# Longer transfer times and margins in a planned instruction order, and six bursts of value products a group for seven

## The reference

```python
x = x + 0.5 * ffn(layernorm(x))
x = x + attn(layernorm(x))
x = x + 0.5 * ffn(layernorm(x))
# ffn:  r = sigmoid(xr @ W_r.T); k = xk @ W_k.T; out = r * (relu(k)**2 @ W_v.T)
#       xr, xk mix each token with the one before it
# attn: q, k, v of 16 heads; rope(q), rope(k); softmax(causal(q k^T / 4)) @ v; @ W_proj + b_proj
```

## Time and profile before

| what | value |
| --- | --- |
| median of 3 runs | 3101.86 us (3099.11 to 3105.67) |
| the profiled execution's own time | 3100.36 us |
| its span, first to last instruction | 3098.6 us |
| PE busy / weight loads busy | 2952.3 us (95%) / 1671.2 us (54%) |
| DVE, ACT, POOL busy | 2497.6 (81%), 2219.9 (72%), 1590.9 us (51%) |

### The profile page before, as it was taken

One profiled execution on the slowest core, in us unless ns is written; L12 is line 12 of the kernel. 1 busy time (PEld: TensorE's weight loads), 2 busy tenths in 40 slices (PEclk: granted clock), 3 DMA queues, 4 the chain that ended last, 5 costly groups with the idle time before them and its releaser, 6 DMA issues.

```text
span 3098.6 us, 56240 instructions
## 1 busy us (share of the span) xinstructions
PE 2952.3 (95%) x18245; PEld 1671.2 (54%) x18245; DVE 2497.6 (81%) x7302; ACT 2219.9 (72%) x4802; POOL 1590.9 (51%) x2190
## 2 busy tenths in 40 slices
PE   6899999999999999999999999999999999999997
PEld 4454455554555545555555555555555555555444
DVE  3888788787878888888888878888888888888872
ACT  4477677777767777777777777777777777777764
POOL 5455455555545555545555555554555555555323
PEclk9899999999999999999999999999999999999999
DMA  3432342333423323333333423323333433433321
GB/s 99 80 78 66 72 96 60 94 75 69 98 59 94 84 67 97 77 84 73 95 74 75 97 61 93 86 75 87 77 87 74 96 71 74 100 67 78 79 63 39
DMA packets 202585, 245.49 MB, mean 79 GB/s; under 512 B 68405, under 2 KB 104245, under 8 KB 202293
## 3 DMA queue, kind: packets, MB, share of 16 engines
q1 hardware_dynamic: 202293, 241.90, 33.5%
HBM read 53.48 MB, written 51.38 MB: 34 GB/s over the span
## 4 chain that ended last, share of the span: by engine, by line
PE 57%; DVE 14%; DMA 8%; ACT 6%; SPq 5%; POOL 5%; issue 4%; POOLq 0%; ACTq 0%; DVEq 0%
PE ps_y L947 11%; PE ps_s L916 11%; PE ps_m L926 9%; PE ps_d L1000 5%; PE ps_d L1003 5%; PE ps_d L1006 5%; DMA sw_sb<-qb_sb 5%; DVE ps_m L1155 4%; PE ps_d L1012 4%; SPq L824 3%; ACT pt_sb L1042 3%; PE ps_d L993 3%; DMA out<-x_sb 3%; DVE mx_sb L1158 2%; DVE ka_sb L1180 2%
## 5 line engine op out<-in xcount | busy, mean ns | idle before, releaser
L1042 ACT ACTIVATE pt_sb<-ps_s 128x512 f32<-128x512 f32 (+1 forms) x3039 | 1455.7, 491 | 703.6 <-PE ps_s L916 675.1
L1155 DVE CUSTOM_DVE_ANT_0 ps_m<-ps_m,mask_sb 128x128 f32<-128x128 f32 (+3 forms) x2048 | 993.7, 497 | 227.7 <-PE ps_m L926 208.8
L926 PE MATMUL ps_m<-kr_sb,qr_sb 96*128 96x512 bf16 (+3 forms) x3072 | 1001.2, 329 | 69.5 <-DVE mx_sb L1155 62.3
L916 PE MATMUL ps_s<-qr_sb,kr_sb 99*128 99x512 bf16 (+1 forms) x3039 | 995.9, 330 | 26.9 <-ACT pt_sb L1042 17.4
L1158 DVE TENSOR_REDUCE mx_sb<-ps_m 128x1 f32<-128x512 f32 x1024 | 700.3, 684 | 91.2 <-PE ps_m L926 83.9
L1287 POOL TENSOR_SCALAR_AFFINE_SELECT pt_sb<-pt_sb 128x512 f32<-128x512 f32 x512 | 337.8, 660 | 580.3 <-ACT pt_sb L1042 578.4
L947 PE MATMUL ps_y<-pt_sb,v_sb 128*32 128x512 f32 (+3 forms) x6144 | 591.9, 495 | 2.9 <-POOL pt_sb L1287 1.9
L916 PEld LDWEIGHTS ps_s<-qr_sb,kr_sb 99*128 99x128 bf16 x3039 | 292.4, 96 | 446.6 <-issue 234.8
L926 PEld LDWEIGHTS ps_m<-kr_sb,qr_sb 96*128 96x128 bf16 x3072 | 302.1, 98 | 378.3 <-DVE mx_sb L1155 111.3
L1000 PE MATMUL ps_d<-ka_sb,wk_sb 128*128 128x256 f32 x1024 | 313.2, 393 | 8.7 <-DVE ka_sb L1180 5.8
L1012 PE MATMUL ps_d<-axn_sb,wqk_sb 128*128 128x256 f32 x1024 | 310.5, 388 | 3.9 <-ACT axn_sb L1084 3.8
(11 more groups left out here) (96 smaller groups left out, 3496.5 us busy)
## 6 DMA issues: line engine op xcount, KB each, us to landing
kr_sb<-part_sb SPq DMA_DIRECT2D x378, 128.0 KB, 3.4
qr_sb<-part_sb SPq DMA_DIRECT2D x378, 128.0 KB, 4.0
y_way<-yt_sb SPq DMA_DIRECT2D x128, 256.0 KB, 2.3
sw_sb<-qb_sb SPq DMA_DIRECT2D x496, 64.0 KB, 2.3
x_sb<-x SPq DMA_DIRECT2D x64, 256.0 KB, 3.3
yn_sb<-y_way SPq DMA_DIRECT2D x64, 256.0 KB
den_sb<-r_way SPq DMA_DIRECT2D x64, 256.0 KB
out<-x_sb SPq DMA_DIRECT2D x64, 256.0 KB, 2.3
```

What stands on the lines that cost most here:

```text
L916: eng.matmul(score_bank(slot)[:, 0:width], kr_sb[0:KR + NP, n % RS, j, kb * P:(kb + 1) * P], qr_sb[0:KR + NP, n % RS, j, q0:q0 + width], s ...
L926: eng.matmul(ps_m[:, u % NM, 0:width], qr_sb[0:KR, n % RS, j, i * P:(i + 1) * P], kr_sb[0:KR, n % RS, j, piece * QC:piece * QC + width], s ...
L1042: eng.activation(pt_sb[:, buffer, j, column:column + width], score_bank(slot)[:, 0:width], ACT.Exp, scale=SCALE).then_inc(exped, 1)
L1155: eng.tensor_tensor_reduce(ps_m[:, u % NM, 0:width], ps_m[:, u % NM, 0:width], mask_sb[:, m0:m0 + width], 1.0, -3e38, ALU.add, ALU.max, be ...
```

## The change

The list gets other numbers, and the bursts another grouping:

- `BURSTS`: the first two ticks of a group form one burst, as the others already do.
- `TAKES`: the times after which a DMA's result is taken to be there grow: `r_swap` 3600 to 7000, `store` 2500 to 5000, `load` 3800 to 7000, `m_rows` 2500 to 3000, `y_out` 3500 to 8000, `y_back` 2700 to 4500, `y_in` 4500 to 9000, and for `rows` and `part` 4900 to 7000.
- `MARGIN`: from slot 192 to slot 3024 a step is ready only so many ns after its inputs are due: PE 0, ACT 200, DVE and POOL 400, SP 1500.
- A step that follows another on the same engine no longer waits for that one's `done` but for the time at which the engine is free again (names with `+`): `f_x1`, `f_k1`, `f_r1`, `a_x1`, `r_b1`, and the steps of `rows` and `part` among themselves.

```diff
-BURSTS = [(0,), (1,), (2, 3), (4, 5), (6, 7), (8, 9), (10, 11)]
+BURSTS = [(0, 1), (2, 3), (4, 5), (6, 7), (8, 9), (10, 11)]
...
-             "a_xn": (477, 645), "a_vc": (477, 645), "a_bias": (1222, 1330), "r_b0": (356, 530), "r_b1": (356, 530), "r_swap": (240, 3600),
+             "a_xn": (477, 645), "a_vc": (477, 645), "a_bias": (1222, 1330), "r_b0": (356, 530), "r_b1": (356, 530), "r_swap": (240, 7000),
...
-             "r_low": (1170, 1500), "store": (60, 2500), "load": (60, 3800), "h_fin": (700, 900), "h_T": (130, 400), "h_copy": (156, 330),
-             "h_rows": (240, 2500), "m_fin": (900, 1000), "m_T": (130, 400), "m_copy": (157, 330), "m_rows": (60, 2500),
-             "y_copy": (477, 645), "y_out": (120, 3500), "y_recip": (159, 300), "y_back": (60, 2700), "y_in": (120, 4500),
+             "r_low": (1170, 1500), "store": (60, 5000), "load": (60, 7000), "h_fin": (700, 900), "h_T": (130, 400), "h_copy": (156, 330),
+             "h_rows": (240, 2500), "m_fin": (900, 1000), "m_T": (130, 400), "m_copy": (157, 330), "m_rows": (60, 3000),
+             "y_copy": (477, 645), "y_out": (120, 8000), "y_recip": (159, 300), "y_back": (60, 4500), "y_in": (120, 9000),
...
-            s("DVE", "f_k1", p, 0.62, t, ("f_k0", p, 0))
+            s("DVE", "f_k1", p, 0.62, t, ("f_k0+", p, 0))
...
-                  (f"rows{t - 1}", n if t else -1, 0))
+                  (f"rows{t - 1}+", n if t else -1, 0))
...
+    MARGIN = {"PE": 0, "ACT": 200, "DVE": 400, "POOL": 400, "SP": 1500}
...
-            if early > slot or not self.ready(now, after) or e != "PE" and rank[0] == 2 and self.TAKES[name][0] > room:
+            if early > slot or not self.ready(now - self.margin(e, slot), after) or e != "PE" and rank[0] == 2 and self.TAKES[name][0] > room:
...
-            pace, seen = self.TAKES.get(key[0], (240, 4900))
+            pace, seen = self.TAKES.get(key[0], (240, 7000))
             self.at[e][slot].append(key)
             self.slots[key] = slot
+            self.done[key[0] + "+", key[1]] = now + pace
             self.done[key] = now + seen
...
+    def margin(self, e, slot):
+
+        return self.MARGIN[e] if BSLOTS <= slot < self.nb * BSLOTS - GSLOTS else 0
...
+                at += self.margin(e, slot)
```

More of the change, by code:

```diff
@@ L152, in describe @@
             s("ACT", "f_x0", p, 0.36, t, ("f_rstd", p, 4))
-            s("ACT", "f_x1", p, 0.36, t, ("f_x0", p, 0))
+            s("ACT", "f_x1", p, 0.36, t, ("f_x0+", p, 0))
             s("PE", "f_T", p, 0.5, t, ("f_x1", p, 2))
@@ L157, in describe @@
             s("DVE", "f_k0", p, 0.62, t, ("f_dif", p, 2), ("f_V", p - 2, 1))
-            s("DVE", "f_k1", p, 0.62, t, ("f_k0", p, 0))
+            s("DVE", "f_k1", p, 0.62, t, ("f_k0+", p, 0))
             s("DVE", "f_r0", p, 0.46, t, ("f_k1", p, 0))
-            s("DVE", "f_r1", p, 0.46, t, ("f_r0", p, 0))
+            s("DVE", "f_r1", p, 0.46, t, ("f_r0+", p, 0))
             s("PE", "f_K", p, 4, t, ("f_k1", p, 3))
@@ L181, in describe @@
                 s("ACT", "a_x0", i, 0.36, t, ("a_rstd", i, 4))
-                s("ACT", "a_x1", i, 0.36, t, ("a_x0", i, 0))
+                s("ACT", "a_x1", i, 0.36, t, ("a_x0+", i, 0))
                 s("PE", "a_T", i, 0.5, t, ("a_x1", i, 2))
@@ L196, in describe @@
                     s("ACT", "r_b0", i, 0.36, t, ("r_QK", i, 1), ("r_low", i - 2 if i >= NCH + 2 else -1, 1))
-                    s("ACT", "r_b1", i, 0.36, t, ("r_b0", i, 0))
+                    s("ACT", "r_b1", i, 0.36, t, ("r_b0+", i, 0))
                     s("SP", "r_swap", i, 3.2, t, ("r_b1", i, 1), ("r_add", i - 1 if i > NCH else -1, 1))
@@ L211, in describe @@
                 if n == 0:
[L212 removed]
+                    s("SP", f"part{t}", n, 1, FIRST + t, (part, NCH // 2 - 1, 2), (f"part{t - 1}+", n if t else -1, 0))
                 s("SP", f"rows{t}", n, 1.6, max(FIRST, at - 2 * GSLOTS + (20 if n == 1 else 1) + 3 * t), (part, last, 2),
[L214 removed]
+                  (f"rows{t - 1}+", n if t else -1, 0))
             if n == 0:
@@ L448, in place_early @@
         for key, slot in self.slots.items():
-            self.done[key] = (slot - SWITCH) * self.TICK + self.TAKES.get(key[0], (240, 4900))[1]
+            self.done[key] = (slot - SWITCH) * self.TICK + self.TAKES.get(key[0], (240, 7000))[1]
             self.done[key[0] + "+", key[1]] = self.done[key] - 3 * self.UNIT
```

## The result

The changed kernel takes 3075.63 us (3071.78 to 3078.87, 4 runs), the kernel before 3100.49 (4 runs): a ratio of 0.9921 [0.9897, 0.9946], 25 us less where 65 were forecast. The lines of after are 7 higher than those of before (916 is now 923, 926 is 933, 1155 is 1162, 1158 is 1165, 1209 is 1216). The profiled execution took 3078.87 us.

A forecast was written before the change was run, and what follows sets the result against it. PE was taken as the bound, with holes made by other engines and transfers. Bursts -14, swap -42, `y_out` -4, clock -8, margins -9 and latency +12 gave -65: 3036 us, range 3005 to 3090.

The forecast's parts named there:

- The transfers: Longer swap times end DVE's waits for swapped halves, and PE's waits for the maxima behind them: -42, between 0 and 84.5 us.
- the one that proves it wrong: Sign against the prediction: DVE's wait for the swap goes, but PE's time per image does not.
- The bursts: Merging a group's first two ticks saves PE 0.24 us in each of 64 groups: 14 us, between 0 and 15.
- Rival (a): Only the bursts count; swaps still land late or the hole moves to POOL's cosine: 3068 to 3083, say 3078; chance 0.20.
- The margins (-9): Margins on ACT, DVE, POOL and SP shorten small waits on neighbours that reach PE: -9 us, between 0 and -45.
- The added latency (+12): Later placement in the list makes some PE slots lose their dense unit: +12 us, between 0 and +70.
- the 20 that were named: Sign against the prediction: PE's waits for lines 1000, 1003 and 1006 grow beyond 20 us.
- rival (b): Slower: later placements empty PE's slots of dense units, 4.5 a group costing 130 us: 3155; chance 0.08.
- no cost: `m_rows`, planned 2.0 us later from a place some 8 us ahead of its use, was to cost nothing.
- The clock (-8): Part of PE's 16 us of full speed missing from 300 to 1100 us returns: -8, between 0 and -16.
- The one event of the forecast: Swap issued at 313.38 us: DVE stands 6.79 us, PE idles 4.17, clock then lower, 3 us more from 320 to 330.
- The tail (0, -3 to +6): Last image's projections move behind the last burst, but scores end sooner by as much: 0, between -3 and +6 us.

The follow-up runs named there:

- the lightened kernels: DVE takes each maximum over half its columns: kernel after 3015.85 us, the same with seven bursts 3012.96, kernel before 3038.02.
- steps without meaning: `HEARD_PE`, when PE's results count as seen, changed from 200 by 10 or 20 ns, order only: old list moved 47 and 82 us, new up to 47.
- the bursts alone: Kernel before with six bursts a group, its list laid out anew by the old times: 3288.51 us, 1.0628 of before.
- six bursts at 210: Changed kernel with `HEARD_PE`, when PE's results count as seen, 210 ns for 200: 3056.83 us, 0.9859 of before.
- seven at 190: Changed kernel with seven bursts and `HEARD_PE`, when PE's results count as seen, 190 ns for 200: 3024.26 us, 0.9773 of before.
- three draws: `HEARD_PE` at 190, 200 and 210 ns in each list: old list's mean 3143.7 us, new list's 86 (seven bursts) and 74 (six) below.

## Why the prediction was wrong

**The transfers: right in what goes, wrong in what it is worth.** The forecast asked for under 15 us of DVE's wait for the swap (0.9) and 0.99 to 1.00 of clock from 300 to 1100 us (1.00); both came. It asked for under 20 us of PE's idle time for DVE and 181 us for an image's scores; 38.9 and 183.2 came. The step that failed is "nearest to PE's own 45.8 us on DVE, which is how much of DVE's 70.0 us reached it. I take 42". It took nearly all of PE's idle time for DVE as made by transfers, and let it go without asking what DVE would do then. By the timelines 26 to 37 of the 46.3 us did stand beside a wait of DVE for a DMA, and all of those went; by the lightened kernels it was some 27, and 19 of them went. What the forecast put at nothing came in their place: 38.9 us of waits for a DVE that is busy. Measured on PE, the term is 7. The sentence that DVE has 16% free was read as room; but the share is a mean, and before the holes of after DVE is busy for 96%. That is nearly the case which the forecast itself named as the one that proves it wrong: DVE's wait went, and PE's time for an image hardly moved (185.1 to 183.2).

By the Trainium skill ("DMA: Bandwidth & Descriptors", section "Anatomy of one DMA") the fixed cost of about 2.0 us and the bytes leave nothing for longer times to gain. The runs part the two questions: the waits that this fit does not see were real and are gone, and what that is worth in time no run shows by itself: `r_swap` alone made the kernel 2.8% slower, within what steps without meaning do to that list.

**The bursts: 14 us only at an order laid out for them.** 1.64 us for 16 records is right, and at the order of after the two single bursts cost 15 us more, as forecast. What failed is "The copies, DMAs and selects are not moved by it": the change lays the list out anew, and PE's new pace moves all of it. Against the list laid out for seven, six are worth +53, +5 and -21: no sign; and at an order laid out for seven they cost 7 and 20. Rival (a), "Only the bursts count", gave 3078, near the time measured, but its premise fell: the swaps did not land late, the hole did not move on to POOL's cosine (189.0 to 29.4 us), and the list alone gives the gain. That its number came so near is luck.

**The margins (-9)** are not to be seen: without them the time is the same within the intervals. **The added latency (+12)** is not either: PE waits 1.9 us for the key product's input, where it was 5.6, and no other product comes near the 20 that were named. So rival (b) fell. One item charged at "no cost" is seen: `m_rows`, planned 2.0 us later. PE now waits 5.0 us in 5 scores for the rows of maxima (`qr_sb<-mt_sb`), for which it had no wait from 300 to 3000 us before.

**The clock (-8).** Right from 300 to 1100 us: 0.98 to 1.00 is 16 us of full speed, the far end of the term. But 0.95 to 0.90 in the first 300 us is 15 lost. Why the head lost it is open: after and the bursts alone show 0.90 there and the order of before with six bursts 0.91, but six bursts at 210 show 0.94 and seven at 190 show 0.92. The one event of the forecast was read a little wrong: the clock falls within the hole, at 324 us, and not behind it, so that part of the 3 us counted there was idle anyway; 2 us more follow from 330 to 340 (last section).

**The tail (0, -3 to +6)** cost 4.8 us from the last group's first score to the end (73.7 before, 78.5 after) and 6.6 from its last score on: about its upper bound of 6. The projections do come behind the last burst, as foreseen; the relief of the scores ahead of them that was to pay for it did not come. PE's timeline of after:

```profile
3024.45 0.86 PE L954 MATMUL ps_y<-pt_sb,v_sb 128*32 128x256 f32 x16 [1.50 <-POOL pt_sb L1294]
3025.69 5.38 PE L1000 MATMUL ps_d<-wp_sb,yn_sb 128*128 128x256 f32 x16 [0.38 <-POOL yn_sb L1346]
```

The burst waits 1.50 us for its select, where it waited 0.69 with projections ahead of it, and the 16 projections follow in one piece.

**The sum again.** One way from before to after can be walked in runs: the order of after with seven bursts is 10 us faster than before, and the six bursts at this order give 15. The second step is the forecast's burst term; the first is the list, for which -51 was forecast. By the traces of before and of that first step it holds -5 (PE's idle time for DVE, 46.3 to 41.1), -4 (the key product's input), -16 (clock from 300 to 1100 us), +6 (clock of the first 300 us, 0.95 to 0.93), +3 (PE's waits for the rows of maxima) and +5 (from the last score on): -11, near the 10. These readings overlap, and 0.01 of the clock is 8 us in 800, so the agreement proves little. The other way, bursts first at the order of before, goes +7 and then -32 by the ratios: the parts are not additive.

**What stays open** is how much of the 25 us is the change and how much the draw. By the means of three draws the change is worth 74 us; the kernel before is 43 better than its mean and the one after 6 worse than its own, which leaves the 25. Three draws a list suggest it and don't prove it. Nor is it shown which placement makes 3024 us of 3071: the trace says only that PE's idle time for DVE is 7.9 us there and 31.8 here.

## What to carry to other kernels

Before you price a wait that goes, ask whether the engine behind it has room in that very stretch: here an engine that was 85% busy in the mean was full where its steps stood in a heap, and gave the bound's engine short waits for long ones. Where a planner writes the order, measure an edit against steps that mean nothing (here 10 ns, up to 82 us) and over several draws, or at an order held fixed. The best of the meaningless neighbours of the new list lies 76 us below the kernel before, three times as far as the changed kernel.

## What the runs showed of the hardware

The same bytes took more DMA time in the new list, which packs the row copies. SP's timeline of before, where pairs of row copies stand some 4 us apart, and of after, where the twelve of a group go out in one piece:

```profile
1522.85 0.61 SPq L839 DMA_DIRECT2D kr_sb<-part_sb  x1
...
1527.09 0.57 SPq L839 DMA_DIRECT2D kr_sb<-part_sb  x1
```

```profile
1505.90 0.61 SPq L846 DMA_DIRECT2D kr_sb<-part_sb  x1
1506.56 0.59 SPq L846 DMA_DIRECT2D qr_sb<-part_sb  x1
...
1513.76 0.60 SPq L846 DMA_DIRECT2D qr_sb<-part_sb  x1
```

Over the execution the packets of 241.90 MB take 39.8% of the DMA engines' time, and 33.5% before; a row copy of 128 KB lands after a median of 4.8 us, and 3.7 before, while a swap's copy lands after 2.0, and 2.2 before. With seven bursts it is 4.8 too, with `r_swap` alone 3.8: so the rows' new spacing or the other times do it, and which is not shown. An estimate from the Trainium skill ("DMA: Bandwidth & Descriptors", section "Anatomy of one DMA"), whose fit for another issuing path is 2.0 us and the bytes at 436 GB/s, would be 2.3 us for 128 KB; neither list's trace agrees. No wait of PE in after is put down to a row copy; the list gives them 7.0 us.

In the kernel before, the clock fell in a long hole of PE and stayed down after it. In the hole of the earlier trace rows PE stands still from 321.5 us to 325.6. In stretches of 1 and 2 us the granted clock is 1.00 up to 324 us, 0.51 from 324 to 325 and 0.50 (1.2 GHz) from there to 334. The 10 us behind the earlier trace rows, columns as there:

```profile
330.00:340.00 10.00, 10.00 (x46) 5.29 (x45) 5.07 (x17) 5.19 (x9) 3.48 (x3) 0.79 0.01 1
```

Over the two long stretches the clock was lower where such holes were longer: 0.97 and 0.96 with holes of up to 7.7 us on PE (bursts alone), 0.99 in both with up to 6.9 (`r_swap` alone), 1.00 in both with up to 3.0 (the new list with seven bursts) and with up to 1.4 (after), with the same products in all. PE's idle time in all falls alike (175, 106, 51 and 58 us from 300 to 3000 us), so that it is the length which counts is suggested and not shown.
